# One VectorE subtraction of the first attention layer moved two places forward in each turn's hand-written order

## What is computed

```python
q = (query @ wq).reshape(bs, s, 32, 128)     # 32 query heads
k = (key @ wk).reshape(bs, s, 8, 128)        # 8 key/value heads, each serves 4 query heads
v = (value @ wv).reshape(bs, s, 8, 128)
q = _rope(q); k = _rope(k)                   # x * cos + rot * sin
scores = einsum(q, k) / sqrt(128)            # per batch 64 x 64, masked
w = softmax(scores)
out = einsum(w, v) @ wo                      # added to x
```

## Time and profile before

| what | value |
|---|---|
| median of 3 runs | 2460.76 us (2460.69 to 2462.11) |
| the profiled execution | 2460.69 us |
| its span, first to last instruction | 2458.9 us |
| busy share PE / DVE / ACT / POOL | 97% / 66% / 51% / 50% |
| mean granted clock of TensorE | 0.991 of full speed |
| layer 0's steady turns | about 336 to 910 us of the span |

### The profile page before, as it was taken

The page is one execution under the profiler, slowest core; times in us unless marked ns, Lnnn a source line. Parts: engine busy times, 40 slices in busy tenths (PEclk is TensorE's granted clock), DMA queues, the critical chain, the costliest instruction groups (busy, mean ns, idle before and its releaser), DMA issues.

```text
span 2458.9 us, 45205 instructions
## 1 busy us (share of the span) xinstructions
PE 2378.6 (97%) x17711; PEld 1306.7 (53%) x17719; DVE 1630.3 (66%) x3133; ACT 1253.9 (51%) x2425; POOL 1220.4 (50%) x981
## 2 busy tenths in 40 slices
PE   7799999999999999999999999999999999999998
PEld 4455555555555555444444555555555555555554
DVE  6877777777777778754444556667666666755666
ACT  6665555555555554533232554555455555544444
POOL 3566666666666666423222364454444445445541
PEclk9899999999999999999999999999999999999999
DMA  6011211111111111101100111122221212221101
GB/s 208 27 44 35 53 44 44 35 44 44 36 53 27 41 21 45 35 18 52 35 28 12 44 31 27 27 61 53 52 58 39 61 36 61 52 42 27 27 14 69
DMA packets 221554, 108.16 MB, mean 44 GB/s; under 512 B 174080, under 2 KB 197280, under 8 KB 221344
## 3 DMA queue, kind: packets, MB, share of 16 engines
q1 hardware_dynamic: 221344, 105.27, 17.0%
HBM read 61.62 MB, written 4.19 MB: 27 GB/s over the span
## 4 chain that ended last, share of the span: by engine, by line
PE 53%; DVE 4%; POOL 3%; ACT 2%; issue 1%; DVEq 0%; ACTq 0%; POOLq 0%
PE PB L854 14%; PE PB L806 12%; PE PB L966 9%; PE PB L790 6%; PE PB L983 5%; PE PB L896 2%; PE PB L831 2%; PE PB L875 1%; DVE AR L2108 1%; DVE SML L1919 1%; PE PB L925 1%; POOL AR L2720 1%; PE PB L1080 0%; POOL PSP L2699 0%; DVE X L2123 0%
## 5 line engine op out<-in xcount | busy, mean ns | idle before, releaser
L854 PE MATMUL PB<-WB,AR 128*128 128x512 f16 x3072 | 691.8, 381 | 24.8 <-DVE X L2123 18.0
L806 PE MATMUL PB<-XTB,WB 128*128 128x512 f16 x3072 | 682.0, 379 | 3.4 <-ACT WB L1352 1.9
L854 PEld LDWEIGHTS PB<-WB,AR 128*128 128x128 f16 x3072 | 296.8, 98 | 388.4 <-DVE X L2123 28.3
L806 PEld LDWEIGHTS PB<-XTB,WB 128*128 128x128 f16 x3072 | 299.1, 98 | 341.9 <-issue 3.1
L2692 POOL TENSOR_TENSOR AR<-AR,SML 128x512 f32<-128x512 f32 x128 | 144.6, 1151 | 316.7 <-DVE SML L2093 316.7
L2123 DVE SCALAR_TENSOR_TENSOR X<-PB,SML,X 128x512 f32<-128x512 f32 x256 | 187.4, 748 | 164.3 <-PE PB L854 158.2
L1476 ACT ACTIVATE AR<-PB 128x512 f16<-128x512 f32 x256 | 131.6, 598 | 239.7 <-PE PB L896 239.7
L2681 POOL TENSOR_TENSOR AR<-AR,CST 128x512 f32<-128x512 f32 x128 | 180.6, 1411 | 44.2 <-ACT AR L1386 44.2
L2003 DVE TENSOR_TENSOR AR<-PB,AR 128x512 f16<-128x512 f32 x128 | 88.2, 690 | 170.3 <-ACT AR L1439 170.3
L966 PE MATMUL PB<-XTB,AR 128*128 128x512 f16 (+1 forms) x864 | 192.5, 379 | 0.0
L1392 ACT ACTIVATE AR<-AR 128x512 f16<-128x512 f32 x128 | 80.5, 630 | 199.1 <-POOL AR L2686 197.6
(11 more groups left out here) (272 smaller groups left out, 3797.6 us busy)
## 6 DMA issues: line engine op xcount, KB each, us to landing
STG<-in_wo SPq DMA_DIRECT2D x14, 1024.0 KB
STG<-in_wq SPq DMA_DIRECT2D x13, 1024.0 KB
STG<-in_qw_gu SPq DMA_DIRECT2D x40, 128.0 KB
STG<-in_ctxT SPq DMA_DIRECT2D x4, 1024.0 KB
X<-in_x SPq DMA_DIRECT2D x4, 1024.0 KB, 10.5
out_x<-X SPq DMA_DIRECT2D x16, 256.0 KB, 2.4
AR<-PSP SPq DMA_TRANSPOSE x240, 2.4
STG<-in_wk SPq DMA_DIRECT2D x14, 256.0 KB
```

Of the source, the lines that this page charges most:

```text
L806: m = pe.do.matmul(b[:, :], wq[x][:, k, h * 128:(h + 1) * 128], XT[y][c][:, k, :], start=n == 0, stop=n == 11)
L854: m = pe.do.matmul(b[:, :], AT[x][:, h, t * 128:(t + 1) * 128], wo[y][:, h, :], start=n == 0, stop=n == 11)
```

## The change

In DVE's `units(L)` the condition on the moved call changes from t == 2 to t == 0. Nothing else changes. In each of the 31 turns of layer 0 the low half of head 3 of the next unit now comes after addition t = 0 and its side work (slot 5), and ahead of additions 1, 2 and 3 and of slots 6 to 8. Before, it came after addition 2 and slot 7. Neither its data nor any signal changes.

```diff
@@ -2477,7 +2477,7 @@
                         if L and t == 2:
                             norm_q(u + 1)
                         side(L, u, 5 + t)
-                        if L == 0 and t == 2:
+                        if L == 0 and t == 0:
                             queries_0(u + 1, 3)
                     side(L, u, 9)
```

## The result

The changed kernel takes 2486.93 us (median of 4 runs, 2485.86 to 2488.18) against 2461.44 us before (4 runs). The ratio is 1.0102, 95% interval 1.0090 to 1.0114, a difference of 25.5 us. The forecast was 2486.0 us.

The account below looks back on a forecast made before the run. A loop through DVE, POOL and ACT, not PE's work, was taken to bound layer 0's steady turns. The terms 8.0 + 4.7 + 7.3 + 5.3 = 25.3 us on 2460.69 us gave 2486.0 us, range 2478 to 2497.

Parts of the forecast that it names:

- What bounds the kernel: Steady turns of layer 0: a loop through DVE, POOL and ACT holds PE once a turn; PE idle 15.1 us.
- The new times after H: Steady turns: weigh starts at about H + 2.1, a new PE stall of 1.35 to 1.45 us a turn.
- H: End of ACT's high half of head 3 in a turn, from which the forecast tells all times; 458.57 in turn 12.
- Kind (a): Ten of turns 8 to 27, with a 512-wide weight piece: 0.8 us later a turn, 8.0 us, bounds 0.7 and 1.35 a turn.
- Kind (c): Five of turns 8 to 27, without a weight piece: everything after weigh moves by the full 1.45 us, 7.3 us in all.
- Kind (b): Five of turns 8 to 27, with a 256-wide weight piece: 0.93 us a turn, 4.7 us in all, bounds 1.5 and 7.3.
- The other eleven turns: Turns 0 to 7 and 28 to 30 of layer 0: together 5.3 us later, 4.9 of it in seven turns.
- Rival 4: TensorE's clock falls with the longer stalls, and the time would pass 2500 us; chance 0.02.

Follow-up runs that it names:

- t == 1: Changed kernel with the low half of head 3 between additions 1 and 2, one addition behind the wait: median 2469.58 us, ratio 1.0028 to the kernel before.
- the order that won 9.8 us: Against the changed kernel, low half of head 3 after addition 2 but ahead of slot 7: median 2452.74 us, ratio 0.9962 to the kernel before.
- the kernel with two turns moved: Kernel before with the low half of head 3 moved ahead of additions 1 and 2 in turns 1 and 30 alone: ratio 1.0007.

## Why the prediction was right, point by point

- What bounds the kernel. That the steady turns hang on the loop through DVE, POOL and ACT and not on PE's work is shown twice: the full stall of PE is charged only where the loop runs through `weigh`, and with PE's work unchanged another place of the same instruction won 6.8 us, and addition 0 put earlier on top of it 13.3.
- The new times after H. `weigh` at H + 2.10 was to be H + 2.1, in all twenty turns. Its wait for addition 2 appears 29 times in the whole run (3 times in the kernel before), where some 27 was forecast. PE's idle time before output 3 was to stay or shrink to half; it shrank to a third (5.2 of 14.9 us).
- Kind (a), 0.8 a turn, 8.0 in all: measured +8.11 with these turns alone, 8.3 in the second profile of the changed kernel. In turn 12, L2676 moves from H + 11.49 to H + 12.29: 0.70 of it is DVE's later start, and 0.10 the first L2050, which the end of POOL's L2672 holds back (0.78 us in place of 0.69).
- Kind (c), 1.45 a turn, 7.3 in all: measured +7.17 alone, 7.3 in the second profile. Turn 11 after, DVE, then PE and POOL, against the earlier trace rows:

```profile
440.38 2.48 DVE L2108 TENSOR_TENSOR AR<-PB,AR 128x512 f16<-128x512 f32 x4 [0.90 <-ACT AR L1476]
...
438.88 1.49 PE L896 MATMUL PB<-AR 64*128 64x256 f16 x24 [1.37 <-DVE X L2123]
...
445.78 1.80 POOL L2672 TENSOR_TENSOR AR<-AR,CST 128x512 f32<-128x512 f32 x1 [9.67 <-ACT AR L1365]
```

H is 436.78 there. `weigh`, `weighed` and L2672 all stand 1.44 to 1.46 further behind H than before.

- Kind (b) is the term that was mis-sized: 4.7 forecast, 2.7 to 2.8 measured. The forecast left the meeting of POOL's L2672 and DVE's L2050 as a tie and took the middle of the two outcomes. DVE won it, in all five turns. Turn 13 after, DVE, then POOL, against the earlier trace rows:

```profile
507.25 1.28 DVE L2050 TENSOR_TENSOR AR<-AR,SML 128x512 f32<-128x512 f32 x2
508.45 0.20 DVE L1855 TENSOR_SCALAR SML<-SML 128x1 f32<-128x1 f32 x1
...
507.28 2.39 POOL L2672 TENSOR_TENSOR AR<-AR,CST 128x512 f32<-128x512 f32 x1 [9.66 <-ACT AR L1365]
509.74 1.26 POOL L2676 TENSOR_TENSOR AR<-AR 128x512 f32<-128x512 f32 x1
```

DVE begins 0.03 us ahead, and its two L2050 take 1.28 us in place of 1.92. POOL's L2672 takes 2.39 in place of 1.27, and L2676 follows it directly: in narrow turns POOL, no longer DVE, ends the wait, so 10 waits are left of 15. Both outcomes had been priced as if DVE ended the wait of L2676. The low one, 0.3, left out that a POOL instruction held back by both L2050 comes last: L2676 moves from H + 10.84 to H + 11.47, which is the 0.63 a turn. In turn 21 it is 0.28, but not for the reason of the low bound: in the kernel before, POOL's L2672 came later there than in the other narrow turns (H + 7.92 in place of 7.55) and L2676 stood at H + 11.20 already. With t == 1 the same happens 0.66 earlier: L2676 starts at H + 10.81, where it was at H + 10.84 before, and so the narrow turns pay nothing. The rule of the Trainium skill (SBUF — State Buffer, section "SBUF: two separate sides") that whoever comes second is blocked holds here with the roles exchanged: 2.39 is 1.12 more than 1.27.
- The other eleven turns: 5.3 forecast, 6.4 in the second profile of the changed kernel (turns 0 to 7 +4.4, turns 28 and 29 +1.5, turn 30 +0.5). Turns 2 and 7 were as worked out (0.43 and -0.14). Turn 30 was 0.5 and not 0.2. The seven turns that were taken to be like (a) at 0.7 each, 4.9 in all, cost 5.5.
- The sum: 18.4 + 6.4 = 24.8 us in the second profile, against 25.3 forecast. The first profile is 25.2 us behind at the last addition of turn 30: 1.0 more by the clock fall in turn 1, 0.6 less in turn 0. Its span is 26.8 us longer; the rest lies behind layer 0. The error in (b), 1.9 too much, and that in the other turns, 1.1 too little, cancel in part, and single runs of a kernel differ by some 3 us. So it is luck that forecast and median agree within 1 us.
- Rival 4 said that the clock might fall with the longer stalls, and was held against because the stall of 1.98 us in turn 30 was longer than the new ones and left the clock alone. Both reasons fail: the new stalls in turns 1 and 30 are 3.62 (2.77 in the second profile) and 2.77 us, and a second profile of the kernel before has a fall at that very place. The falls did come, twice in the first profile; the one in turn 1 cost 1.0 us, and the time stayed far below the 2500 us that the rival named.
- Behind the last addition of turn 30 the span still has 1452.3 and 1453.1 us to run in the two profiles of the kernel before, 1453.9 and 1454.3 in those of the changed one. The nine other kernels lie between 1451.9 and 1454.0, so nothing there has changed beyond the shift, as forecast, as far as such a spread lets one tell. It leaves 1 to 2 us of the whole that the turns don't account for.

## What to carry to other kernels

In an engine that works strictly in order, the price of a wait is set by what stands behind it and who waits for that, not by its length: against its old place the same instruction cost 25 us (after addition 0), 7 us (after addition 1) or minus 10 us (after addition 2, ahead of the side work). Put a waiting instruction after everything whose inputs are already there, and ahead of the first that waits longer. Measure the moment of arrival in the trace first, and look for the loop: an engine that was busy 97% was not the bound here, for its idle time had one name and returned nearly every turn. And look for what the shift will run into: in the narrow turns a meeting of POOL and DVE swallowed both a loss and a gain of 0.3 to 0.4 us.

## What the hardware showed that I had not expected

One POOL instruction that reads and writes SBUF was held back by two DVE instructions on end (2.39 us for 1.27, turn 13), though it had been ready 0.03 us after the first began; in turn 11, where it became ready 0.02 us after the second began, it was held back by that one alone (1.80). Who comes first can decide 0.66 us a turn: with the order that won 9.8 us, DVE came first by 0.23 us in turn 21 and second by 0.12 in turn 13, and POOL's next instruction started 0.66 earlier in turn 21.

TensorE's granted clock went to half for 3.4 us behind idle times of 1.99, 2.00, 2.77 and 3.62 us in some executions. It stayed at full speed behind 2.77 us in another execution, at the same place of the same program, and behind 2.98 us in turn 1 of the kernel with two turns moved.
